# First attention: squares of q and k packed into one tile of 128 rows, and DRAM fills issued in the second attention

## The reference

```
q, k, v = conv(silu(x @ Wq)), conv(silu(x @ Wk)), conv(silu(x @ Wv))   # 4 taps, per channel
q, k = q*cos + rot_half(q)*sin, k*cos + rot_half(k)*sin
q, k = q / max(norm(q), 1e-12), k / max(norm(k), 1e-12)               # norm over the 128 channels of a head
for s in range(4):                                                    # token t looks at t, t-1, t-2, t-3
    out += (sum(q * lag(k, s)) * scale * sigmoid(lag(a, s) * b)) * lag(v, s)
out = out * rms(out) * norm_w * silu(x @ Wz);  y = out @ Wout
```

## Time and profile before

| | us |
|---|---|
| median of three runs | 1094.26 (1093.77 to 1094.26) |
| the profiled execution | 1096.4 |
| its span, from first to last instruction | 1094.6 |
| TensorE busy | 1011.9 |
| VectorE busy | 749.7 |
| ScalarE busy | 554.1 |
| GpSimd busy | 284.2 |

### The profile page before, as it was taken

One profiled execution on the slowest core, in us unless ns is written; L12 is line 12 of the kernel. 1 busy time (PEld: TensorE's weight loads), 2 busy tenths in 40 slices (PEclk: granted clock), 3 DMA queues, 4 the chain that ended last, 5 costly groups with the idle time before them and its releaser, 6 DMA issues.

```text
span 1094.6 us, 16914 instructions
## 1 busy us (share of the span) xinstructions
PE 1011.9 (92%) x5768; PEld 804.6 (74%) x5768; DVE 749.7 (68%) x1303; ACT 554.1 (51%) x1097; POOL 284.2 (26%) x246
## 2 busy tenths in 40 slices
PE   6989999999999999999979999999988996589987
PEld 4778998998899854354468988989885454278876
DVE  4778999899899869972477787877873154423444
ACT  2558877877887788711155565555641123023220
POOL 1034334423433401030112112121100005536660
PEclk9989999999999999989989999999998998789997
DMA  7097867877867940430011011111002002278845
GB/s 224 3 218 152 192 147 158 172 170 154 167 159 167 255 112 0 158 83 0 7 52 58 29 58 46 41 58 29 29 0 73 0 1 87 81 229 271 275 134 196
DMA packets 78461, 121.59 MB, mean 111 GB/s; under 512 B 25091, under 2 KB 54606, under 8 KB 77776
## 3 DMA queue, kind: packets, MB, share of 16 engines
q1 hardware_dynamic: 66384, 86.91, 26.3%
q0 software_dynamic: 12032, 34.11, 15.7%
HBM read 70.31 MB, written 38.08 MB: 99 GB/s over the span
## 4 chain that ended last, share of the span: by engine, by line
PE 79%; DVE 10%; DMA 3%; ACT 3%; issue 3%; POOL 2%; POOLq 0%; SPq 0%; ACTq 0%; DVEq 0%
PE psum L632 9%; PE psum L633 9%; PE psum L634 9%; PE psum L857 5%; PE psum L1040 5%; PE psum L686 5%; PE psum L999 5%; PE psum L804 4%; PE psum L882 3%; PE psum L764 3%; PE psum L745 3%; PE psum L1050 2%; PE psum L813 2%; PE psum L675 2%; DVE arena L1492 2%
## 5 line engine op out<-in xcount | busy, mean ns | idle before, releaser
L1492 DVE SCALAR_TENSOR_TENSOR arena<-arena,par_in 128x1024 f32<-128x1024 f32 x144 | 183.5, 1283 | 33.3 <-ACT arena L1122 23.6
L632 PE MATMUL psum<-G_r,arena_r 128*128 128x512 f32 x320 | 132.7, 415 | 7.2 <-DVE G_r L1585 4.1
L633 PE MATMUL psum<-G_r,arena_r 128*128 128x512 f32 x320 | 127.9, 400 | 0.0
L634 PE MATMUL psum<-G_r,arena_r 128*128 128x512 f32 x320 | 127.5, 399 | 0.0
L1924 POOL DMA_DIRECT2D arena<-arena x64 | 53.8, 983 | 210.4 <-DVE arena L1504 210.2
L1270 ACT ACTIVATE arena<-psum,small 128x256 f32<-128x256 f32 x128 | 59.3, 473 | 87.3 <-DVE small L1650 87.3
L1112 ACT ACTIVATE arena<-psum 128x1024 f32<-128x1024 f32 x48 | 49.2, 1026 | 62.6 <-PE psum L634 62.0
L632 PE MATMUL psum<-arena_r 128*128 128x256 f32 x256 | 78.0, 305 | 2.2 <-DVE arena_r L1675 1.5
L632 PEld LDWEIGHTS psum<-G_r,arena_r 128*128 128x128 f32 x320 | 61.3, 191 | 21.4 <-DVE G_r L1585 4.9
L1940 POOL TENSOR_TENSOR arena_r<-arena,arena_r 128x512 fp32r<-128x512 f32 x16 | 20.7, 1293 | 214.5 <-ACT arena_r L1239 214.5
L1973 POOL DMA_INDIRECT out_rows<-arena x64 | 62.2, 973 | 47.7 <-DVE arena L1825 25.3
(11 more groups left out here) (238 smaller groups left out, 2375.1 us busy)
## 6 DMA issues: line engine op xcount, KB each, us to landing
arena<-arena POOLq DMA_DIRECT2D x64, 256.0 KB, 5.6
arena<-in_w_moe SPq DMA_DIRECT2D x33, 384.0 KB, 3.7
slot_rows<-nowhere SPq DMA_DIRECT2D x16, 576.0 KB, 4.4
arena<-slot_rows SPq DMA_DIRECT2D x32, 288.0 KB, 3.8
arena<-bands SPq DMA_DIRECT2D x16, 528.0 KB, 4.3
sq_rows<-arena POOLq DMA_DIRECT2D x16, 512.0 KB, 7.4
arena<-in_w_qkvz SPq DMA_DIRECT2D x16, 384.0 KB, 3.7
arena<-in_qkv_codes SPq DMA_DIRECT2D x16, 384.0 KB, 3.2
```

The lines of the kernel that those rows point to most:

```text
L632: nc.tensor.matmul(dst, w_l, x_h, start=start, stop=False, skip_group_check=True)
L633: nc.tensor.matmul(dst, w_h, x_l, start=False, stop=False, skip_group_check=True)
L634: return nc.tensor.matmul(dst, w_h, x_h, start=False, stop=stop, skip_group_check=True)
L1492: nc.vector.scalar_tensor_tensor(by_batch(dst), by_batch(u[s])[:, :, j:j + S], par_in[:, bass.ds(M_CW + (w * H + h) * TAPS + j, 1)], by_ba ...
```

## The change

The squares of q and of k of a head end up in one tile `sqq` of 128 rows: 64 rows of q's, each the sum of two channels' squares, and 64 rows of k's.

1. ScalarE squares q whole into `sqq`. GpSimd then adds the upper 64 rows to the lower 64 by DMA (semaphore `a0_fold`).
2. ScalarE squares the lower 64 channels of k into `sqk`, waits for `a0_fold`, and squares the upper 64 into the upper 64 rows of `sqq`. GpSimd adds `sqk` to them by a second DMA (`a0_sq_qk`). Both squares of k now stand ahead of `v_tok`; the one square of k stood behind it.
3. TensorE multiplies each 128 tokens of `sqq` by `by_pair`, whose column 0 is one in the lower rows and whose other columns are one in the upper rows: 8 matmuls give both sums, where 16 did. They stand at the head of the turn; the eight between the scores and `project_q` are gone.
4. VectorE sets `by_pair` once (four memsets) and copies the sums in their new order.
5. The fills of `slot_rows` (576 KB) and `out_rows` (256 KB) leave the 16 turns of the first attention; SyncE issues one pair behind the weights of each head of the second attention.

```diff
@@ -124,7 +124,7 @@
         nowhere, nil = sb("nowhere", ROW), sb("nil", D)
         lut_idx = lut_w.bitcast(I32)
         ident, ones, inv_d = cst[:, C_ID:C_ID + P], cst[:, C_ONE:C_ONE + P], cst[:, C_INV:C_INV + P]
-        strict = cst[:, C_STRICT:C_STRICT + P]
+        strict, by_pair = cst[:, C_STRICT:C_STRICT + P], cst[:, C_MASK:C_MASK + P]
         half_scale, seam = 0.5 * SCALE, cst[:, C_SEAM:C_SEAM + PAD]
         cos_t, sin_t = cst[:, C_COS:C_COS + S], cst[:, C_SIN:C_SIN + S]
         iota_e, tok_id = cst[:, C_IOTA:C_IOTA + E], cst[:, C_TOK:C_TOK + NT]
@@ -510,10 +510,6 @@
                     if par:
                         sp.wait_ge(sg("a0_z"), h + 1)
                         load_z(hh + 1)
-                sp.dma_start(slot_rows.rearrange("(h p r) c -> h p r c", h=H, p=P)[h],
-                             nowhere.unsqueeze(1).broadcast_to([P, SLOTS // (H * P), ROW])).then_inc(sg("moe_fill"), 16)
-                sp.dma_start(out_rows.rearrange("(h p r) c -> h p r c", h=H, p=P)[h],
-                             nil.unsqueeze(1).broadcast_to([P, T * TOPK // (H * P), D])).then_inc(sg("moe_fill"), 16)
 
             sp.wait_ge(sg("pool_fill"), 1)
             sp.dma_start(sq_rows.rearrange("p (r c) -> p r c", c=D), nil.unsqueeze(1).broadcast_to([P, T // D, D]))\
@@ -554,9 +550,18 @@
             for g in range(4):
                 sp.dma_start(wo_s[32 * g:32 * g + 32, :], a["wo_scales"][g:g + 1, :].broadcast_to([32, H * D]))\
                     .then_inc(sg("in_wo"), 16)
+
+            def fill(h):
+                sp.dma_start(slot_rows.rearrange("(h p r) c -> h p r c", h=H, p=P)[h],
+                             nowhere.unsqueeze(1).broadcast_to([P, SLOTS // (H * P), ROW])).then_inc(sg("moe_fill"), 16)
+                sp.dma_start(out_rows.rearrange("(h p r) c -> h p r c", h=H, p=P)[h],
+                             nil.unsqueeze(1).broadcast_to([P, T * TOPK // (H * P), D])).then_inc(sg("moe_fill"), 16)
+
+            fill(0)
             with sp.Fori(1, H) as h:
                 sp.wait_ge(sg("a1_wmul"), h)
                 load1(h)
+                fill(h)
 
             sp.wait_ge(sg("a1_o"), H)
             for e in range(WRING):
@@ -680,16 +685,16 @@
                 def project0(dst, j, n):
                     return halves0(dst, par, j, n)
 
-                def squared_sums(j, s):
+                if 2 in st:
+                    if is_last(h, 1):
+                        pe.wait_ge(sg("a_sb"), 7)
+                    pe.wait_ge(sg("a0_sq_qk"), 16 * h)
+                    if since(h, 2):
+                        pe.wait_ge(sg("a0_ssq_s"), h - 1)
                     for i in range(NT):
-                        n = j * NT + i
-                        m = nc.tensor.matmul(bank(7)[:, n:n + P], sqr[s][:, i * P:i * P + P], ones,
+                        m = nc.tensor.matmul(bank(7)[:, 2 * i:2 * i + P], sqq[:, i * P:i * P + P], by_pair,
                                              start=True, stop=True, skip_group_check=True)
-                    return m
-
-                if 2 in st:
-                    pe.wait_ge(sg("a0_sq_k"), h)
-                    squared_sums(1, "k").then_inc(sg("a0_ssq"), 1)
+                    m.then_inc(sg("a0_ssq"), 1)
                 if 1 in st:
                     if since(h, 1):
                         pe.wait_ge(sg("a0_silu_z"), h)
@@ -747,11 +752,6 @@
                     if is_last(h):
                         pe.wait_ge(sg("in_wout_b"), 16)
                         project_out(0, 0, range(7, 10))
-                if 1 in st:
-                    pe.wait_ge(sg("a0_sq_q"), h + 1)
-                    if since(h, 1):
-                        pe.wait_ge(sg("a0_ssq_s"), h)
-                    squared_sums(0, "q")
                 if 4 in st:
                     project_q(h + 1, 1 - par)
                 if 2 in st:
@@ -1167,14 +1167,22 @@
                                          scale=par_in[:, bass.ds(M_NW + h - 2, 1)]).then_inc(sg("a0_gT_sb"), 1)
                 if 1 in st:
                     silu_and_tap(h, 2, "v", cv[par])
-                def squared(s):
-                    act.wait_ge(sg("a0_conv_" + s), 3 * h + 3)
+                def squared_q():
+                    act.wait_ge(sg("a0_conv_q"), 3 * h + 3)
                     if since(h, 1):
                         act.wait_ge(sg("a0_ssq"), h)
-                    nc.scalar.activation(sqr[s], c_[s], ACT.Square).then_inc(sg("a0_sq_" + s), 1)
-
-                if 1 in st:
-                    squared("q")
+                    nc.scalar.activation(sqq, cq, ACT.Square).then_inc(sg("a0_sq_q"), 1)
+
+                def squared_k():
+                    act.wait_ge(sg("a0_conv_k"), 3 * h + 3)
+                    if since(h, 1):
+                        act.wait_ge(sg("a0_sq_qk"), 16 * h)
+                    nc.scalar.activation(sqk[0:P // 2, :], ck[0:P // 2, :], ACT.Square)
+                    act.wait_ge(sg("a0_fold"), 16 * (h + 1))
+                    nc.scalar.activation(sqq[P // 2:P, :], ck[P // 2:P, :], ACT.Square).then_inc(sg("a0_sq_k"), 1)
+
+                if 1 in st:
+                    squared_q()
                     if is_last(h, 0):
                         tanh_gates()
                     act.wait_ge(sg("a0_z"), h + 1)
@@ -1184,6 +1192,7 @@
                         i = nc.scalar.activation(by_tile(sz[zq][e][:, z_half(par, zq) * 512:z_half(par, zq) * 512 + 512]),
                                                  slot(1).rearrange("p (t e d) -> p e t d", e=2, d=P)[:, e], ACT.Silu)
                     i.then_inc(sg("a0_silu_z"), 1)
+                    squared_k()
                 if is_last(h):
                     lut_act(0)
                 if 2 in st:
@@ -1198,8 +1207,6 @@
                     m.then_inc(sg("a0_v_tok"), 1)
                 if is_last(h):
                     lut_act(1)
-                if 1 in st:
-                    squared("k")
                 if 4 in st:
                     silu_and_tap(h + 1, 0, "q", cq)
 
@@ -1516,7 +1523,9 @@
                     dve.wait_ge(sg("a0_ssq"), h)
                     if since(h, 2):
                         dve.wait_ge(sg("a0_rqk"), h - 1)
-                    nc.vector.tensor_scalar(ssq_s, bank(7)[:, 0:2 * NT], 1e-24, None, ALU.max).then_inc(sg("a0_ssq_s"), 1)
+                    nc.vector.tensor_scalar(ssq_s.rearrange("p (s i) -> p s i", s=2),
+                                            bank(7)[:, 0:2 * NT].rearrange("p (i s) -> p s i", s=2), 1e-24, None, ALU.max)\
+                        .then_inc(sg("a0_ssq_s"), 1)
                 if is_last(h):
                     dve.wait_ge(sg("in_idx"), 32)
                     dve.wait_ge(sg("a0_rs_k"), H)
@@ -1536,6 +1545,11 @@
                     conv(2, "v", cv[par])
                 if is_last(h, 0):
                     gates_scaled()
+                    for q_rows in range(2):
+                        r = slice(0, P // 2) if q_rows else slice(P // 2, P)
+                        nc.vector.memset(by_pair[r, 0:1], float(q_rows))
+                        i = nc.vector.memset(by_pair[r, 1:P], float(1 - q_rows))
+                    i.then_inc(sg("a_sb"), 1)
                 if 2 in st:
                     dve.wait_ge(sg("a0_S"), h)
                     dve.wait_ge(sg(f"a0_band{1 - par}"), 16 * (hh + par))
@@ -1917,6 +1931,11 @@
                         pool.wait_ge(sg("a0_on"), h - 1)
                     nc.gpsimd.tensor_tensor(rqk[1 - par], ssq_s, neg_half, ALU.pow).then_inc(sg("a0_rqk"), 1)
                 if 1 in st:
+                    low, high = slice(0, P // 2), slice(P // 2, P)
+                    pool.wait_ge(sg("a0_sq_q"), h + 1)
+                    nc.gpsimd.dma_start(sqq[low, :], sqq[high, :], accum_op=ALU.add).then_inc(sg("a0_fold"), 16)
+                    pool.wait_ge(sg("a0_sq_k"), h + 1)
+                    nc.gpsimd.dma_start(sqq[high, :], sqk[low, :], accum_op=ALU.add).then_inc(sg("a0_sq_qk"), 16)
                     for s in "qk":
                         pool.wait_ge(sg("a0_rc_" + s), h + 1)
                         pool.wait_ge(sg("a0_rs_" + s), h + 1)
```

## The result

The changed kernel takes 1189.7 us (median of four runs, 1184.5 to 1194.1), against 1094.0 before: a ratio of 1.0868, interval 1.0842 to 1.0894. The profiled execution took 1188.65 us with a span of 1186.9, which is 92.3 more than before. That is slower by 95.7 us in the medians, inside the predicted range of 1140 to 1199 and 14 us above the value of 1176.

A forecast was written before the change was run, and what follows sets the result against it. TensorE was taken as the bound, with little room on other engines. Fourteen turns at +5.65 us (79), turn 15 (+5.2) and the start (-2.8) gave +81.4 on 1096.4: 1178, by median 1176 us; range 1140 to 1199.

The forecast's parts named there:

- The wait: First attention: TensorE idles 5.1 us before `project_q` in each of 14 turns, for `v_tok` held up behind the fold.
- The landing: The first adding DMA, the fold, lands 3.8 us after its issue, with 3.1 and 4.8 as bounds.
- The clock: Behind each gap TensorE runs at half clock for 3.7 to 5.5 us, losing 2.35 us a turn.
- The turn: A steady turn of the first attention grows from 21.30 to 26.95 us, +5.65, in turns 1 to 14: 79 us.
- The start: Turn 1: a new wait replaces the old stall and head 2's weights land sooner: -2.8 us, between 0 and -5.
- Turn 15: No `project_q` there; o starts 2.9 us later behind `v_tok` and loses 2.35 us at half clock: +5.2 us.
- The fills: Moving 832 KB out of each first-attention turn gains nothing in steady turns; the second attention hides them.
- The sum: Whole kernel: 79 + 5.2 - 2.8 = +81.4 us, so 1176 us by median; 65 in 100.
- The removal: Eight sums between scores and `project_q` cost 1.78 us; only 1.0 would come, as 0.8 us of `v_tok` wait replaces them.
- Faster: Rival: `project_q` meets no unfinished `v_tok` and VectorE's 19.5 us, some 20.3 with starts, bounds the turn: 1077 us; 5 in 100.
- that the clock holds: Rival: the gap before `project_q` stays but TensorE keeps full clock, turn 24.6 us: 1140 us; 14 in 100.
- That the fold lands as late as 5.6 us: Rival: the fold lands at the median of 5.6 us, +27 us on the forecast: 1203 us; 14 in 100.

The follow-up runs named there:

- Experiment 1: Changed kernel with both squares of k, and the wait for the fold, behind `v_tok` instead of ahead of it: 1131.5 us, ratio 1.0314.
- experiment 5: Changed kernel with ScalarE writing k's upper square into `sqk` without waiting for the fold; GpSimd waits instead, before the second DMA: 1155.0 us, ratio 1.0525.
- experiment 9: Kernel before the change with the eight sums of q left out and nothing added: 1090.1 us, ratio 0.9939.
- experiment 2: Changed kernel with 20 useless matmuls between the scores and `project_q`, in TensorE's gap: 1162.3 us, ratio 1.0615.
- experiment 3: Kernel before the change with only the fills moved to the second attention, squares as before: 1097.6 us, ratio 1.0000.
- Experiment 6: Changed kernel with SyncE's five large loads of turn 15 waiting for the fold of head 15: 1183.3 us, ratio 1.0800.
- experiment 8: Experiment 7's kernel with the eight sums moved behind the projection of k of the next turn: 1115.6 us, ratio 1.0177 to the kernel before the change.
- experiment 7: Changed kernel with both squares of k behind `v_tok` and the five loads of turn 15 behind the fold: 1123.5 us, ratio 1.0253.

## Why the prediction was right

- **The wait.** Right, in place, number and size. `v_tok` was to end 19.1 us behind o and ended 18.9 behind it in the turn shown and 19.9 in the next, where z's weights travel with the fold (it landed in 4.5 us instead of 3.5). The gap was to be 5.1 us and is 5.5 on average. Experiment 1 shows the place as the cause. Experiments 5 and 9 divide the gap: 2.4 us are the landing, 2.1 the two squares, and 1.0 the wait that the sums had covered.
- **The landing.** Taken as 3.8 us; the median of the folds is 4.0, the shortest 3.5, as in the earlier trace rows. In the steady turns there are two values rather than one, 3.5 us without z's weights and 4.3 to 5.0 beside them; the one value of 3.8 stood for both. The estimate of 2.6 us by the formula of the Trainium skill (DMA: Bandwidth & Descriptors, "Anatomy of one DMA") would have been 1.4 us short, as the earlier trace rows had suggested. The second DMA lands later, 4.8 in the median, which the prediction had no row for; in the changed kernel `project_q` and o cover it, in experiment 1 nothing does.
- **The clock.** Taken as 2.35 us a turn; 2.3 in the turn shown, 2.2 on average (21.7 - 19.5), 1.9 by experiment 2 and 2.1 by its twelve regular turns. The gap of 3.1 us in experiment 5 has the echo as well, which the earlier trace rows left open.
- **The turn.** 27.24 us against 26.95 predicted; 13 turns cost 77.2 us more, where 13 x 5.65 = 73.5 were expected.
- **The start.** Turn 1 ends 2.4 us later than before (82.56 against 80.16), where the terms 5.65 - 2.8 gave 2.85. The sum was right, and one reason in it was not. I expected the weights of head 2 to land sooner without the fills; in the changed kernel they did (6.0 us after their issue), but in experiment 3, where only the fills are moved, they took 8.7, and nothing is gained there.
- **Turn 15.** This term was mis-sized. It was +5.2 us and is +9.5: from the sums of turn 15 to the end of o, 28.6 us against 19.1. The step used the landing of a steady turn, but SyncE issues five large loads at that very moment, and the fold took 8.5 us. Experiment 6 shows it. The clock's part of the term was right in kind: o took 4.7 us there instead of 3.0. The profile of before had these loads, issued behind z of head 15; I read only the steady turns' traffic.
- **The fills.** Costed at nothing, and nothing is what experiment 3 measured. In the second attention the changed kernel takes 1.8 us more from the first projection to the experts' first rows (412.7 against 410.9), of which 1.5 are a longer wait for `slot_rows` at its end. Experiment 3, with the same fills, is not slower, so I leave this open.
- **The sum.** +2.4, +77.2 and +9.5 make 89.1 at the end of turn 15's o. The span grew by 92.3; of the other 3.2 us, 1.8 are those just named and the rest is spread. In the range the upper end adds up to 106 rather than 105, a slip of 1 us.
- **The removal.** The prediction says that of each 1.78 us only 1.0 would come with nothing else changed. Experiment 9 measured 0.57: the wait is 0.97 us instead of 0.8, and the start behind it, for which there was no term, costs 0.24. The sum of the forecast does not rest on this, but the rival "Faster" at 1077 us does, and was put too low.

The rivals: that the clock holds was refuted in this kernel (0.50 behind every gap looked at) and made true in experiment 2, which gives its price. That the fold lands as late as 5.6 us came true in turn 15 alone. Faster was never near: even with the wait for the fold off ScalarE the kernel loses 5%, and with nothing but the gain left in, it wins 0.6%.

## What to carry to other kernels

An engine that is busy all the time can still be covering waits: before taking work out of it, look at what each instruction behind that work waits for, and when that came. Here the eight sums behind the scores hid a wait for `v_tok`, so that 1.78 us removed are worth 0.57, and the eight at the head of the turn hid one for the copy of o. And before putting an instruction with a DMA wait into an in-order queue, list what stands behind it and who waits for that: two squares and their wait in the wrong place of ScalarE's queue cost 58 us here; right behind `v_tok` they leave a loss of 3%.

## What the runs showed of the hardware

- Whether a gap on TensorE brings the low clock is not told by its length alone. Behind 5.5 us in every turn of the changed kernel and 3.1 in every turn of experiment 5 it came in all turns looked at; behind 1.0 to 1.4 us (experiment 8) it never did. Between them both happen: 1.83 us (experiment 2) and 1.84 (experiment 1) had it, 1.82 (experiment 1) and once even 3.18 (experiment 7, sums in 2.05 us) had not. What decides between them is not shown. Filling the gap with useless matmuls made the kernel 2.3% faster.
- In experiment 9 a wait costs more than its length: the first matmul behind it takes 0.47 us in the chain where one in a row takes 0.23 (experiment 9).
- An activation over 64 rows takes what one over 128 takes: 1.05 us for the lower square of k, 1.05 for the whole square of q, so here splitting a square by rows doubles its price.
- Removing 832 KB of fills from each turn, of a DMA share of 0.75, moved the landing of an adding DMA of 256 KB by only 0.5 us; 4.2 MB of loads, issued from 0.6 us ahead of it to 1.4 behind, moved it by 5 (8.5 us, where the same fold takes 3.5 in experiment 6).
